# Gated experts beside sparse attention: expert biases and residual summed by GpSimd, head scores on two row halves

## The reference, cut to what matters

```
x = x + experts(layernorm(x)):
    k_tok   = number of experts of a token, from relu(xf @ dp_w1 + dp_b1) @ dp_w2 (softplus, clip, round)
    logits  = xf @ gate_w + gate_b;  softmax over the k_tok largest -> dense_w [token, 4]
    hid     = relu(xf @ ew1[e] + eb1[e]);   y[e] = hid @ ew2[e] + eb2[e]
    out     = sum over e of dense_w[:, e] * y[e]
then, on layernorm of the new x:
    scores  = Q K^T / sqrt(32) for 4 heads of width 32; the 32 largest of 120 are kept per row and head,
    softmax over them; mean over the heads -> attn_mean;  c_t = attn_mean @ V
    scale_in, shift_in = c_t @ W_film_in + b_film_in;  x_in = layernorm(x) * (1 + gate*scale_in) + gate*shift_in
```

## Time and profile before

| what | value |
|---|---|
| median of 3 runs (lowest, highest) | 4931.16 us (4923.28, 4934.56) |
| span of the profiled execution | 4930.8 us, 90627 instructions |
| its own time beside the span | not listed apart; the span is 0.4 us under the median |
| granted TensorE clock, mean over the span | 0.958 of full speed |
| busy over the whole span | PE 91%, PEld 71%, DVE 65%, ACT 41%, POOL 37% |
| the stage of the change | about 2650 to 3965 us of the span |

### The profile page before, as it was taken

One profiled execution on the slowest core, in us unless ns is written; L12 is line 12 of the kernel. 1 busy time (PEld: TensorE's weight loads), 2 busy tenths in 40 slices (PEclk: granted clock), 3 DMA queues, 4 the chain that ended last, 5 costly groups with the idle time before them and its releaser, 6 DMA issues. The chain is left out here.

```text
span 4930.8 us, 90627 instructions
## 1 busy us (share of the span) xinstructions
PE 4484.1 (91%) x31852; PEld 3484.2 (71%) x31852; DVE 3190.3 (65%) x9752; ACT 2002.6 (41%) x4154; POOL 1819.8 (37%) x2248
## 2 busy tenths in 40 slices
PE   7999769988995999789996999999999977999979
PEld 5666547767884888667774788888888644777856
DVE  6888689967553332178883788888888843444344
ACT  3555357744442322145552334434334332222234
POOL 2222146532454332155540233333333303666533
PEclk9999889988997999899997999999999989999989
DMA  4666512235223222122222011001110083222233
GB/s 116 155 149 153 125 57 70 63 114 168 61 57 74 71 71 69 54 72 68 76 59 74 27 34 28 28 28 29 30 34 24 17 258 106 88 88 87 72 113 105
DMA packets 332892, 391.32 MB, mean 79 GB/s; under 512 B 66485, under 2 KB 301466, under 8 KB 321690
## 3 DMA queue, kind: packets, MB, share of 16 engines
q1 hardware_dynamic: 319130, 360.28, 25.9%
q0 software_dynamic: 13312, 25.25, 2.2%
HBM read 296.33 MB, written 89.10 MB: 78 GB/s over the span
## 5 line engine op out<-in xcount | busy, mean ns | idle before, releaser
L2549 PE MATMUL fa_h<-fa_xnT,fa_w 128*128 128x256 f32 x2048 | 485.4, 383 | 0.0
L2561 PE MATMUL fa_y<-fa_w,fa_hT 128*128 128x256 f32 x2048 | 462.5, 379 | 0.0
L2549 PEld LDWEIGHTS fa_h<-fa_xnT,fa_w 128*128 128x128 f32 x2048 | 380.5, 191 | 81.9 <-issue 27.5
L2561 PEld LDWEIGHTS fa_y<-fa_w,fa_hT 128*128 128x128 f32 x2048 | 386.9, 190 | 65.0 <-issue 15.4
L2424 ACT ACTIVATE fa_hT<-fa_h,fa_b 128x256 f32<-128x256 f32 x512 | 214.6, 470 | 534.5 <-PE fa_h L2549 473.1
L425 DVE TENSOR_REDUCE a_mx<-a_score 128x16 f32<-128x1920 f32 x128 | 276.1, 2157 | 53.4 <-PE a_score L609 53.3
L2942 ACT ACTIVATE m_hT<-m_h,m_b 128x256 f32<-128x256 f32 x256 | 107.4, 470 | 363.2 <-PE m_h L3003 363.2
L1566 PE MATMUL r_h<-r_xnT,r_rw 128*128 128x256 f32 x1024 | 247.3, 390 | 0.7 <-ACT r_xnT L1516 0.7
L1867 ACT ACTIVATE e_hT<-e_h,e_b 128x256 f32<-128x256 f32 x256 | 107.3, 470 | 335.0 <-PE e_h L1921 335.0
L1706 POOL DMA_INDIRECT e_xg<-moe_rows,e_idx x64 | 128.6, 2009 | 307.9 <-issue 254.8
L3003 PE MATMUL m_h<-m_hnT,m_w 128*128 128x256 f32 x1024 | 235.7, 379 | 2.5 <-ACT m_hnT L2932 2.5
(11 more groups left out here) (463 smaller groups left out, 10820.2 us busy)
## 6 DMA issues: line engine op xcount, KB each, us to landing
a_floor<-a_lowest SPq DMA_DIRECT2D x64, 960.0 KB, 8.6
cv_toep<-kernels SPq DMA_DIRECT2D x16, 2048.0 KB, 9.5
x<-a_xo SPq DMA_DIRECT2D x96, 256.0 KB, 4.3
f_xb<-x SPq DMA_DIRECT2D x64, 256.0 KB, 3.0
f_xres<-x SPq DMA_DIRECT2D x64, 256.0 KB, 3.0
a_xb<-x SPq DMA_DIRECT2D x64, 256.0 KB, 3.0
e_w<-in_L_ffn_ew SPq DMA_DIRECT2D x16, 1024.0 KB, 7.6
a_cb<-in_ctx SPq DMA_DIRECT2D x96, 90.0 KB, 2.9
```

Source lines behind the costliest of these rows:

```text
L2549: last = pe.matmul(h_ps[j % 2][:, c, :], w1[:, e, k, f:f + P], xnT[it.p][:, k, :], start=k == 0, stop=k == KD - 1)
L2561: last = pe.matmul(bank[:, t * D:(t + 1) * D], hT[e % 2][:, k, t * P:(t + 1) * P], w2[:, e, k, :], start=k == 0, stop=k == KE - 1)
```

## The change

- The biases b2 are now loaded as [128 x 4 x 256], broadcast to all partitions, instead of [4 x 256].
- turn_weights, wT_out and bias are gone, with their semaphores. VectorE's begin_sum is gone.
- A new begin_sum on GpSimd, with lag 4 and last in its list, multiplies each expert's bias row with the gate weights, adds the four, and adds the residual. VectorE's add_expert(0) and the reuse of buffers wait for its semaphore `begun`. add_expert and down use bank e % 2 of y_ps.
- scores issues four products instead of two: for each row tile, heads 0 and 1 from rows 0 to 63 and heads 2 and 3 from rows 64 to 127, each with 240 columns, into two neighbouring banks. kd holds two heads per half ([128 x 2 x 120]); take_scores reads four pieces of 240 instead of two of 480, after all four products; film_values waits for both tiles' takes.

```diff
-    b2 = st.sb("b2", [NG, D])
+    b2, biased = st.sb("b2", [P, NG, D]), st.sb("biased", [P, TL, D])
-    t_ps, g_ps, a_ps, b_ps = (st.ps(n, [P, 512]) for n in ("t", "g", "a", "b"))
+    t_ps, g_ps = (st.ps(n, [P, 512]) for n in ("t", "g"))
+    ba_ps = st.ps("ba", [P, 2, 512])
+    b_ps, a_ps = ba_ps[:, 0, :], ba_ps[:, 1, :]
+    pair = st.sb("pair", [P, 2])
...
+            sp.dma_start(b2[:].rearrange("p e d -> p (e d)"), w["eb2"].rearrange("e d -> (e d)").partition_broadcast(P)).then_inc(small, 16)
...
             def load_residual(it):
                 if it.reused():
-                    sp.wait_ge(summed, SUM * (it.i - 2) + 1)
+                    sp.wait_ge(begun, it.i - 1)
...
+            pool.tensor_tensor(pair[:], const["heads4"][:, 0:2], const["heads4"][:, 2:4], ALU.add).then_inc(padded, 1)
...
+            def begin_sum(it):
+                p = it.p
+                c = Chain(pool, weighed, it.i, BIAS)
+                pool.wait_ge(gate, GATE * (it.i + 1))
+                if it.reused():
+                    pool.wait_ge(stored[p], 16 * it.h)
+                    pool.wait_ge(xn3_ready, it.i - 1)
+                if it.reused(1):
+                    pool.wait_ge(begun, it.i)
+                for e in range(NG):
+                    out = xo[p] if e == 0 else biased
+                    c.add(pool.tensor_tensor(out[:], b2[:, e:e + 1, :].to_broadcast([P, TL, D]),
+                                             wgt[p][:, :, e].unsqueeze(2).to_broadcast([P, TL, D]), ALU.mult))
+                    c.wait()
+                    if e:
+                        c.add(pool.tensor_tensor(xo[p][:], xo[p][:], biased[:], ALU.add))
+                        c.wait()
+                pool.wait_ge(r_in[p], 16 * (it.h + 1))
+                pool.tensor_tensor(xo[p][:], xo[p][:], xres[p][:], ALU.add).then_inc(begun, 1)
...
-                pool.tensor_tensor(kd[:], kT[:].unsqueeze(1).to_broadcast([P, NH, SK]),
-                                   const["heads4"][:].unsqueeze(2).to_broadcast([P, NH, SK]), ALU.mult).then_inc(kd_ready, 1)
+                pool.tensor_tensor(kd[:], kT[:].unsqueeze(1).to_broadcast([P, 2, SK]),
+                                   pair[:].unsqueeze(2).to_broadcast([P, 2, SK]), ALU.mult).then_inc(kd_ready, 1)
...
             pipeline(pool, B, DEPTH, [
                 (6, roots_of_sum), (6, roots_of_normed), (6, key_mask), (6, affine), (6, spread_k), (7, scale_heads(0)), (7, scale_heads(1)),
-                (6, negate_max(0)), (6, negate_max(1)), (1, roots_of), (7, mix(0)), (7, mix(1))])
+                (6, negate_max(0)), (6, negate_max(1)), (1, roots_of), (7, mix(0)), (7, mix(1)), (4, begin_sum)])
...
             def add_expert(e):
-                    dve.wait_ge(summed, SUM * it.i + e + 1)
+                    if e == 0:
+                        dve.wait_ge(begun, it.i + 1)
+                    else:
+                        dve.wait_ge(summed, SUM * it.i + e)
...
             def take_scores(it):
-                for t, bank in ((0, b_ps), (1, a_ps)):
-                    dve.wait_ge(s_done, 2 * it.i + t + 1)
+                dve.wait_ge(s_done, it.i + 1)
+                for t in range(TL):
...
-                    c.add(dve.scalar_tensor_tensor(sc[t][:], bank[:, 0:NH * SK].rearrange("p (h k) -> p h k", k=SK), (P // NH) ** -0.5,
-                                                   kmf[it.p][:].unsqueeze(1).to_broadcast([P, NH, SK]), ALU.mult, ALU.add))
+                    for half in two:
+                        last = dve.scalar_tensor_tensor(sc[t][:, 2 * half:2 * half + 2, :],
+                                                        ba_ps[:, half, t * 2 * SK:(t + 1) * 2 * SK].rearrange("p (h k) -> p h k", k=SK), (P // NH) ** -0.5,
+                                                        kmf[it.p][:].unsqueeze(1).to_broadcast([P, 2, SK]), ALU.mult, ALU.add)
+                    c.add(last)
...
             pipeline(dve, B, DEPTH, [
-                (6, sum_stats), (7, pick_round(2)), (6, norm_sum), (4, rank_gates), (5, begin_sum), (7, pick_round(3)), (7, keep_taken),
+                (6, sum_stats), (7, pick_round(2)), (6, norm_sum), (4, rank_gates), (7, pick_round(3)), (7, keep_taken),
...
             def scores(it):
-                for t, bank in ((0, b_ps), (1, a_ps)):
-                    pe.matmul(bank[:, 0:NH * SK], qT[:, t * P:(t + 1) * P], kd[:].rearrange("p h k -> p (h k)"),
-                              start=True, stop=True).then_inc(s_done, 1)
+                for t in range(TL):
+                    for half in two:
+                        rows = slice(half * P // 2, (half + 1) * P // 2)
+                        last = pe.matmul(ba_ps[:, half, t * 2 * SK:(t + 1) * 2 * SK], qT[rows, t * P:(t + 1) * P],
+                                         kd[rows].rearrange("p h k -> p (h k)"), start=True, stop=True)
+                last.then_inc(s_done, 1)
...
             def film_values(it):
                 if it.followed(1):
-                    pe.wait_ge(pick, PICK * (it.i + 1) + 1)
+                    pe.wait_ge(pick, PICK * (it.i + 1) + TL)
```

More of the change, by code:

```diff
@@ L2036, in adaptive_with_sparse_attention @@
     GATE = PRE + 14
-    SUM = NG + 1
+    SUM = NG
+    BIAS = 2 * NG - 1
     PAIRS = NG * KE // 2
@@ L2213, in rank_gates @@
                 if it.reused():
-                    dve.wait_ge(w_turned, it.i - 1)
+                    dve.wait_ge(begun, it.i - 1)
                     dve.wait_ge(summed, SUM * (it.i - 1))
@@ L2267, in weigh_gates @@
                 assert c.n == GATE
[L2269 to L2282, removed]
             def add_expert(e):
@@ L2380, in step @@
                     bank = (a_ps, b_ps)[t]
-                    dve.scalar_tensor_tensor(film[t][:], bank[:], mod[:, 0:1], bf[:], ALU.mult, ALU.add).then_inc(film_ready, 1)
+                    dve.scalar_tensor_tensor(film[t][:], bank, mod[:, 0:1], bf[:], ALU.mult, ALU.add).then_inc(film_ready, 1)
                 return step
             pipeline(dve, B, DEPTH, [
-                (6, sum_stats), (7, pick_round(2)), (6, norm_sum), (4, rank_gates), (5, begin_sum), (7, pick_round(3)), (7, keep_taken),
+                (6, sum_stats), (7, pick_round(2)), (6, norm_sum), (4, rank_gates), (7, pick_round(3)), (7, keep_taken),
                 (7, weigh_heads(0)), (7, weigh_heads(1)), (4, weigh_gates), (7, sum_heads(0)), (7, sum_heads(1)), (5, add_expert(0)), (6, take_scores), (6, pick_round(0)),
-                (5, add_expert(1)), (4, wT_out), (1, norm_stats), (7, film_out(0)), (6, pick_round(1)), (2, norm), (5, add_expert(2)),
+                (5, add_expert(1)), (1, norm_stats), (7, film_out(0)), (6, pick_round(1)), (2, norm), (5, add_expert(2)),
                 (7, film_out(1)), (5, add_expert(3))])
@@ L2509, in difficulty @@
                 if it.reused(1):
-                    pe.wait_ge(wT_ready, it.i)
+                    pe.wait_ge(gate, GATE * (it.i - 1) + 2)
                 for k in range(KD):
@@ L2522, in gates @@
                 last.then_inc(g_done, 1)
-            def turn_weights(it):
-                pe.wait_ge(gate, GATE * (it.i + 1))
-                for t in range(TL):
-                    last = pe.transpose(g_ps[0:NG, t * P:(t + 1) * P], wgt[it.p][:, t, :], const["ident"][:])
-                last.then_inc(w_turned, 1)
-            def bias(it):
-                pe.wait_ge(wT_ready, it.i + 1)
-                if it.reused(1):
-                    pe.wait_ge(summed, SUM * it.i - 1)
-                for t in range(TL):
-                    last = pe.matmul(y_ps[it.p][:, t * D:(t + 1) * D], wT[:, t * P:(t + 1) * P], b2[:], start=True, stop=True)
-                last.then_inc(b_done, 1)
             def up(j):
@@ L2622, in step @@
                     bank = (a_ps, b_ps)[t]
-                    pe.matmul(bank[:], aT[:, t * P:(t + 1) * P], vf[:], start=True, stop=True).then_inc(f_done, 1)
+                    pe.matmul(bank, aT[:, t * P:(t + 1) * P], vf[:], start=True, stop=True).then_inc(f_done, 1)
                 return step
             pipeline(pe, B, DEPTH, [
-                (4, difficulty), (5, up(0)), (4, gates), (5, up(1)), (5, up(2)), (5, bias), (5, up(3)), (6, turn_sum),
-                (5, up(4)), (5, down(0)), (6, fold), (6, project), (5, down(1)), (6, scores), (5, up(5)), (4, turn_weights), (7, film_values), (5, up(6)), (7, mean_heads),
+                (4, difficulty), (5, up(0)), (4, gates), (5, up(1)), (5, up(2)), (5, up(3)), (6, turn_sum),
+                (5, up(4)), (5, down(0)), (6, fold), (6, project), (5, down(1)), (6, scores), (5, up(5)), (7, film_values), (5, up(6)), (7, mean_heads),
                 (5, up(7)), (7, film_in(0)), (3, turn_x), (5, down(2)), (7, film_in(1)), (5, down(3))])
```

22 lines of the change are left out of this document (11 added, 11 removed).

## The result

| kernel | median us (lowest, highest) | profiled span | granted clock |
|---|---|---|---|
| before, beside it | 4930.0 (4923.28, 4934.56) | 4930.8 | 0.958 |
| changed | 5048.09 (5044.72, 5056.62) | 5054.8 | 0.947 |

The ratio is 1.024, 95% interval 1.0226 to 1.0255; the forecast was 5047 us. The stage of the change, up to the next stage's first product, is 117.7 us longer (4090.69 against 3973.00), about the difference of the medians. The profiled execution of the changed kernel is the slowest of its four, and the other 6.3 us of its span lie behind the stage, where the kernels are the same. First the window that answers to the earlier trace rows: TensorE, busy at 100% before, is idle for 8% of the time, and GpSimd went from 34% to 52%.

A forecast was written before the change was run, and what follows sets the result against it. TensorE was taken to set the pace before, and a loop through GpSimd's begin_sum after the change. Loop +105, clock +20 and edges -9 gave +116 us on 4931, so 5047 us, range 5005 to 5110.

The forecast's parts named there:

- the loop: norm_sum, takes, film_values, film_out, mix(1), begin_sum, roots_of_sum, next norm_sum: 42.4 us a slot against 38.77, 29 times, +105 us.
- The place of the wait: VectorE idle 5 us before the normalisation of fa_xo (norm_sum), released by GpSimd, where nothing waited before.
- the eight durations: begin_sum on GpSimd: four multiplications of 1.05 us, four additions of 1.26 and eight gaps of 0.07, sum 9.8 us.
- the 1.0 us of the scores: Score products on TensorE: 8 records on overlapping row halves take 1.0 us instead of 1.62; bounds 1.0 and 1.8.
- the two stops: TensorE stands still 5.5 us per slot: 3 us before film_values and 2.5 us before turn_sum.
- the clock: TensorE's clock falls at film_values in half of the slots, losing about 1.4 us each: 0.7 us per slot, +20 us.
- the edges: Stage start -6, bias load +2, slots 5 and 6 -1.3 each and -0.6, slot 36 -2: together -9 us.
- a fall at turn_sum costs nothing, since the film_values stall takes it up: TensorE's clock falling at turn_sum adds no time, as the later stall before film_values absorbs it.
- the faster rival: begin_sum is hidden and TensorE stays the bound: -64 us, 4867 us; chance 0.08.
- the loop without it is 32.6 us, so it decides at 38.77 - 32.6 = 6.2 us for the eight instructions: Point at which begin_sum on GpSimd becomes hidden: 6.2 us for its eight instructions, 0.77 us each.
- the bounds of the port: VectorE and GpSimd holding each other up in SBUF: nothing added, bounds 0 and +1.3 us per slot.
- TensorE's part: TensorE's work per slot: bias products 1.06, transposes 0.22 and scores 0.6 us less, 1.9 together, to 36.9 us.

The follow-up runs named there:

- early: The changed kernel with begin_sum moved in GpSimd's list from last place to just before the two negate_max steps; 4869.82 us, ratio 0.987 to the kernel before.
- more: The changed kernel with four more multiplications in begin_sum, into a tile nobody reads; 5169.25 us, ratio 1.0478 to the kernel before.
- fill: The changed kernel with two TensorE products per slot that nobody reads, just before film_values; 5075.32 us, ratio 1.0193 to the kernel before.
- two: The changed kernel with only the biases of experts 0 and 1 added (4 GpSimd instructions, not 8); 4986.58 us, ratio 1.0108 to the kernel before.
- middle: The changed kernel with begin_sum behind key_mask and ahead of affine and spread_k, lag 5 instead of 4; 5133.26 us, ratio 1.0315 to the kernel before.
- scores: The kernel before with only the score products on row halves, biases and residual as before; ratio 0.9973 to the kernel before, slots of 38.37 us.
- early_bias: The changed kernel with scores as in the kernel before and begin_sum before negate_max in GpSimd's list; ratio 0.9914 to the kernel before, slots of 37.30 us.

## Why the prediction was right, and where it was not

**Right: the loop.** Its terms beside those of the slot above:

| step | predicted us | measured us |
|---|---|---|
| norm_sum to film_values | 16.95 | 16.89 |
| film_values to film_out(0), full clock | 6.5 | 9.91 less 3.4 of clock |
| film_out(0) to film_out(1)'s end | 6.3 | 6.35 |
| mix(1) | 1.7 | 1.66 |
| begin_sum | 9.8 | 9.76 |
| roots_of_sum and handover | 1.1 | 1.06 |

Undisturbed that is 42.2 us against the 42.4 forecast. 29 slots of 43.06 us give 29 x 4.29 = +124 us; the forecast had 105 + 20 = +125. The place of the wait, the eight durations, the 1.0 us of the scores (3025.21 to 3026.22), VectorE's wait (5 us, 4.98 measured) and the two stops (3 and 2.5 us predicted, 2.56 and 2.33 measured) came as written. TensorE's busy share, put near 86%, is 92% in the window, as products at the lower clock count as busy for longer. That the order and not the amount of work is the cause is shown by early, and the slope by more. That the total came within 1 us is luck: the loop was put 6 us too high, the clock 5 too low and the edges 2 too low.

**Right in sum, not in form: the clock.** It was put at 1.4 us in half of the slots. It was 3.4 us in 5 of 29 slots, 1.7 in three, and 0 to 0.7 in the others: (43.06 - 42.2) x 29 = 25 us against 20. In the short slots the step "a fall at turn_sum costs nothing, since the film_values stall takes it up" is what the rows show; in five others (42.7 to 42.9) some 0.5 us is lost before film_values. fill shows the clock by itself: its slots lack the long kind and the ratio falls from 1.024 to 1.0193, 23 us.

**Off in size: the edges.** The start gave -8.1 us at norm_sum of the seventh slot (2756.22 against 2764.32 us), close to the steps named (-4, -1.3 twice and -0.6); the end, from norm_sum of slot 36 on, cost 0.9 us where -2 was put. The first statistics of the stage, whose input is loaded behind the biases, start 1.0 us later (2656.73 against 2655.73), where 2 were put for the bias load. Together -7 instead of -9.

**Wrong: the point from which the faster rival decides.** The step "the loop without it is 32.6 us, so it decides at 38.77 - 32.6 = 6.2 us for the eight instructions" failed, and with it the 4867 us below that point. It takes the 32.6 us as fixed. In two begin_sum is 4.82 us and the slot 41.07, so the rest of the same loop is 36.25 us: 2.1 us more for keep_taken, held by affine, and 1.7 us for the clock. In the one slot where keep_taken came first the rest is 32.9 us. Nor would less of begin_sum help much while they meet in that order: VectorE's own way round is only 0.1 us shorter. And at its best, in early, that second way has 0.2 us to spare: the takes end 16.45 us behind norm_sum, and film_values starts at 16.68. So what holds VectorE there for longer than that, or lowers TensorE's clock on the way, is paid almost in full. What puts affine ahead in two is, by an estimate from these rows, begin_sum itself: affine starts 2.5 us behind turn_sum in both kernels, and turn_sum 3.36 us behind norm_sum in early and 3.24 in two, where norm_sum is 0.1 us late. No run with a still shorter begin_sum tests this.

**Wrong: the bounds of the port.** "Add nothing (bounds 0 and +1.3 us per slot, one long instruction)" held at 0 for the changed kernel (L136 0.73, L2366 1.22 us; L2270 is held for 0.8 us in some slots, as L2264 was before). As a bound it fails: two shows 2.1 us in keep_taken alone, middle about 4 us. The prediction listed the VectorE steps beside begin_sum where it stands, and not what becomes of the meeting of affine and keep_taken, which its own rows show, when the one that comes first changes. The Trainium skill, SBUF — State Buffer, section Who interferes with whom, says that copies, casts and tensor_scalar can take the shared port pair, and instructions with two SBUF inputs too. The traces agree: in middle it is a CAST, TENSOR_SCALARs of two elements and SCALAR_TENSOR_TENSORs that wait, while the MAX8 between them keep their 0.27 us.

**Off in size: TensorE's part, with the right sum by luck.** scores was expected to gain 18 us and gained 13 (0.4 us a slot, not 0.6). The term left out what the scores do to their neighbours: down ahead of them takes 3.54 us from start to start and not 3.45 (3008.30 to 3011.84 in scores), and up behind them 1.83 and not 1.73. So the changes to and from the row halves cost 0.2 us more than the 0.2 that the prediction took. The bias products and the transposes, put at 1.28 us, were worth 1.47 (38.77 to 37.30 in early_bias), since the 24 products of up around the bias products fell from 5.46 to 5.27 us as well. 1.47 + 0.40 gives the 1.9 us of the prediction.

## What to carry to other kernels

An engine at 34% can hold the whole pipeline: before moving work to it, follow the loop through its list, from the new step to the first step behind it that somebody waits for, and back. A point from which an edit becomes free, worked out from such a loop, holds only while the rest of the loop keeps its length. So close the other loops too, and where two engines share a port, look at which pairs of long steps meet and by how little the first one leads: here 0.1 us decided over 2 us and the clock behind it. Pieces from a step to itself one slot later always add up to the slot; what binds is told by the waits.

## What the runs showed that was not expected

- Of two equal stops of TensorE at turn_sum, 2.33 us each, the first left the clock at 2.4 GHz and the second brought it to 1.2 GHz; the stop at film_values that followed the first then cost 3.4 us more than itself. Products that nobody reads, put into that stop, took 23 to 54 us off the program.
- A TENSOR_SCALAR of 128x2 elements takes 0.17 us alone and 0.84 to 0.99 beside a long GpSimd instruction.
- In early and in two, who starts first by some tenths of a microsecond, GpSimd's affine or VectorE's keep_taken, makes a slot of 36.9 into one of 41.1 us, and one of 41.07 into one of 37.7.
- One edit changed its sign: the row halves were worth -0.27%, +0.6% and -0.44%, by what set the pace.
